# Issuing the stores of the kept dense tiles from ScalarE's queue instead of SyncE's

## The chip, the cores and the metric

The kernel runs on one core of one Trainium2 chip. The metric is the device time of one execution in microseconds (us); the lower, the better. The kernel before was timed three times, and its median is what the changed kernel is compared with. Engines are named TensorE (PE in the profile), VectorE (DVE), ScalarE (ACT), GpSimd (POOL) and SyncE (SP).

## The reference, cut to what matters

Two graph layers run on 6,250 nodes of 128 features. The 106,250 edges are sorted by destination.

```
edge_index = stack([src, dst])
h = relu(layernorm(x));  x = x + GCN(h)      # two convolutions; each gathers rows by src,
                                             # scales them and sums them by dst
h = relu(layernorm(x));  x = x + CFConv(h)   # filter from edge_attr (64 -> 128 -> 128),
                                             # times gathered rows, mean by dst, two linear layers
```

The kernel folds the two weight matrices of the first layer into one, so that what is left of that layer is twice the same thing: out[dst] += table[src] over all edges. These are the first and the second pass. The third pass is the edge filter of the second layer.

## The kernel before, in words

**Two ways to sum.** The 208 groups of 512 edges are sorted by destination. Of every 13 groups, 7 make a dense tile: a matrix of counts between all source nodes (49 blocks of 128) and the 232 destination columns from the tile's first destination on. Such a tile is summed by multiplying the table, held in SBUF as three bf16 parts, with this matrix (`multiply`, L2078). The groups outside tiles are summed by gathering their rows with GpSimd (L1019) and multiplying them with a one-hot matrix (`sum_window`, L2012).

**Building a tile.** A tile has 28 chunks of 128 edges. For each chunk VectorE makes one-hot codes (L1585), TensorE counts them into PSUM (`count_chunk`, L2035 and L2040), and ScalarE copies the counts into the matrix `adjacency` (`copy_chunk`, L1178). The counts have two PSUM places, so TensorE may count chunk m when chunk m-2 has been copied (`wait(pe, chunk_copied, m - 1)`). `adjacency` has two buffers. Before a tile is built, ScalarE zeroes the last columns of its buffer (`clear`, L1157).

**Kept tiles.** 12 of the 16 tiles (`KEPT`) are built in the first pass and needed again in the second. Each is stored to HBM in 7 pieces of 406 KB (`keep`, L787), and loaded again in the second pass (`load_tile`, L798). The store adds to `tile_kept[b]`; for that semaphore `clear` waits when the buffer is to be used again, and SyncE waits once before the second pass.

**The order of the work.** The first pass has 124 slots, one for each group that is gathered. A plan written before anything runs says what belongs to each slot: about 3 chunks of the next tile, a third of a slot's product pieces between them, one or two `pack` steps of the edge attributes for the third pass, and at times a node update. Each engine goes through the slots in order and takes its own part of each, so all five keep in step by semaphores alone. Tiles begin about every 9 slots: the slot in which a tile's last 4 chunks are copied ends with ScalarE's `clear` for the tile that is begun, and has no product on TensorE. The pieces to keep stand in the four slots after that one (2, 2, 2 and 1 pieces):

```
for i in range(PARTS):
    plan.keeps.setdefault(at[t + 1] + 1 + i // 2, []).append((t, i))
```

**SyncE in a slot of the first pass:** loads of edge attributes (`load_attr`, L769, after a wait for TensorE's `packed`), then the pieces to keep (each after a wait for `chunk_copied`), then the store of packed attributes (L781) and the store of the last updated row block (`store_row`, L746).

**ScalarE in a slot of the first pass:** the fields of the next pack (`edge_fields`, L1207), the register loads of the chunks' columns (L1166), the first chunk's copy, `pack_out` (L1221, four copies of 67x64, with its own register loads at L1215), the other chunks' copies, at three places in the pass a zeroing of a packing buffer (L1202, 3.1 us), and `clear` where the plan has one.

**The second and the third pass** have their own loops; the change does not touch their code.

Of the kernel before, what the change touches and what calls it, by code (L numbers as in the profile page):

```python
# [26 lines left out]
COLS = 232  # L27
TILE_GROUPS = 7
TILE_CHUNKS = TILE_GROUPS * CHUNKS
# [48 lines left out]
def gnn_kernel(nc, x, src, dst, edge_attr, edge_weight, W1, b1, W2, b2,  # L78
# [178 lines left out]
    with ExitStack() as ctx:  # L257
# [416 lines left out]
        def _(sp):  # L674
# [106 lines left out]
                sp.dma_start(packed_attr[:, run * SUPER:(run + 1) * SUPER],  # L781
                             packed_T[0:R, run % 2, 0:SUPER]).then_inc(attr_stored[run % 2], 16)

            def keep(t, i):
                b = buffer_of(1, KEPT[t])
                sp.wait_ge(chunk_copied, TILE_CHUNKS * (t + 1))
                sp.dma_start(kept_tiles[t][:, i * BP * COLS:(i + 1) * BP * COLS],  # L787
                             adjacency[:, b, i * BP:(i + 1) * BP, :].rearrange("p b n -> p (b n)")
                             ).then_inc(tile_kept[b], 16)

            def load_tile(order, i):
                t = KEPT.index(PLAN[2].tiles[order])
                before = LOADED.index(order)
# [23 lines left out]
            def fast_path():  # L817
                store_inverse(0)
                for c in (1, 2):
                    plan = PLAN[c]  # L820
                    before = -1
                    if c == 2:
                        sp.wait_ge(block_used[1], NB * len(KEPT))
                        for b in range(2):
                            sp.wait_ge(tile_kept[b], 16 * PARTS * len([t for t in range(len(KEPT)) if t % 2 == b]))
                        wait_stored(sp, 2)
                        load_table(PARTS - 1)
                        sp.wait_ge(inv_stored, 16)
                        load_x(2, 0)
                        for i in range(PARTS):  # L830
                            load_tile(LOADED[0], i)
                    for n in range(SLOT_COUNT[c]):
                        for q in plan.attrs.get(n, []):
                            load_attr(q)
                        for piece in plan.keeps.get(n, []):
                            keep(*piece)
                        if c == 1 and n == max(plan.adds):
                            for i in range(PARTS - 1):
                                load_table(i)
                        for piece in plan.loads.get(n, []):  # L840
                            load_tile(*piece)
                        if n in plan.ends:
                            store_packed(plan.ends[n])
                        if c == 1 and n - 1 in plan.updates:
                            store_row(1, plan.updates[n - 1])
                        if c == 2 and n in plan.updates:
                            j = plan.updates[n]
                            if j:
                                store_mid(j - 1)
                                store_row(2, j - 1)  # L850
                            if j + 1 < NB:
                                load_x(2, j + 1)
                        if c == 2 and n == LAST_PACK_SLOT + 4:
                            for b in range(2):
                                sp.wait_ge(attr_stored[b], 16 * SUPERS // 2)
                            sp.wait_ge(packed_read, SUPERS)
                            late_params()
                        if c == 2 and n == SLOT_COUNT[2] - REST_SLOTS + 2:
                            sp.wait_ge(block_used[2], NB * TILES)
                            for i in range(2):  # L860
                                load_piece(i)
                    if c == 1:
                        left = [plan.updates[SLOT_COUNT[1] - 1]] if SLOT_COUNT[1] - 1 in plan.updates else []
                        for j in left + plan.tail:
                            store_row(1, j)
                    else:
                        first = NB - len(plan.tail)
                        for j in range(first - 1, NB):
                            if j >= first and j + 1 < NB:
                                load_x(2, j + 1)  # L870
                            store_mid(j)
                            store_row(2, j)
# [184 lines left out]
        def _(act):  # L1057
# [135 lines left out]
            def split_middle(b):  # L1193
                source, parts = half_blocks(b)
                act.wait_ge(rest_ready, b + 1)
                nc.scalar.copy(parts[1], source).then_inc(middle_ready, 1)

            def zero_packed(run):
                if run >= 2:
                    act.wait_ge(attr_stored[run % 2], 16 * (run // 2))  # L1200
                    act.wait_ge(packed_read, run - 1)
                nc.scalar.copy(packed_T[:, run % 2, :], zeros[0:RF, 0:1].to_broadcast([RF, WIDE])  # L1202
                               ).then_inc(packed_zero, 1)
# [46 lines left out]
            def fast_path():  # L1250
# [3 lines left out]
                for c in (1, 2):  # L1254
# [3 lines left out]
                    for n in range(SLOT_COUNT[c]):  # L1258
# [36 lines left out]
                        if c == 1 and n in (PARTS, PARTS + 1):  # L1295
                            if n == PARTS:
                                act.wait_ge(parts_ready, 2 * PARTS)
                            zero_packed(n - PARTS)
                        if n in plan.clears:
                            clear(plan.clears[n])  # L1300
                last = SLOT_COUNT[2] - 1
# [1014 lines left out]
```

## Time and profile before

| what | value |
|---|---|
| median of 3 runs | 1527.09 us (1525.73 to 1532.16) |
| profiled execution, first to last instruction | 1923.0 us |
| PE busy | 1426.5 us |
| POOL busy | 1110.3 us |
| DVE busy | 826.7 us |
| ACT busy | 692.3 us |
| mean granted clock of TensorE | 0.850 |

The profiled execution is 396 us longer than the median of the runs; there is no other time of it than this span. So a time from the trace is one of a slower execution: a sum of such times stands against 1923.0 us, and has to be brought to 1527.09 us (a factor of 0.794) before it says anything of the metric. Matmuls are pipelined, and their ends are modelled, so a busy TensorE is not one at its peak. Instructions that load registers, wait, or issue DMAs are not counted as busy; the rows call them ACTq or SPq.

### The profile page before, as it was taken

To read this page: it belongs to the slowest core of one execution; us is meant where nothing else is said; L and a number is where in the kernel's file an instruction comes from. 1 tells how busy PE (TensorE), PEld (TensorE's weight loads), DVE (VectorE), ACT (ScalarE), POOL (GpSimd) and SP (SyncE) were. 2 spreads that over 40 slices of the span, in tenths; PEclk is the share of its full clock that TensorE was granted. 3 is DMA by queue.
4 is the path that set the end of the run, shared out by engine and by line. 5 is a ranking of instruction groups with operands and counts; after the bars stand their busy time and mean duration, and the time that the engine had idled before them with its cause. 6 is when DMAs were issued, how large, how long until landed. Compare 5 with 4: busy or idle time off the path is not lost.

```text
span 1923.0 us, 36276 instructions
## 1 busy us (share of the span) xinstructions
PE 1426.5 (74%) x12042; PEld 1188.7 (62%) x12042; DVE 826.7 (43%) x2907; ACT 692.3 (36%) x1947; POOL 1110.3 (58%) x1150
## 2 busy tenths in 40 slices
PE   3247777888788788885677777767777477888887
PEld 1246666777677676774567666666666345565665
DVE  4854434455445554444133334333333324444444
ACT  3645545555445555442243223322331011111111
POOL 7666656555655655653655555565555645556552
PEclk9856999888988988886899878988998668788887
DMA  3324344444344434447466645664564522344321
GB/s 102 85 52 119 91 118 145 132 133 118 97 130 145 133 110 107 130 132 219 114 162 182 179 125 147 173 183 124 164 179 112 127 63 66 90 98 97 90 71 49
DMA packets 248261, 235.42 MB, mean 122 GB/s; under 512 B 137443, under 2 KB 207512, under 8 KB 247173
## 3 DMA queue, kind: packets, MB, share of 16 engines
q1 hardware_dynamic: 206853, 148.54, 27.9%
q0 software_dynamic: 41216, 84.48, 16.4%
q8 instruction: 101, 1.65, 0.4%
q14 instruction: 91, 0.75, 0.1%
HBM read 173.22 MB, written 59.68 MB: 121 GB/s over the span
## 4 chain that ended last, share of the span: by engine, by line
PE 51%; another core or an unknown queue 15%; issue 12%; DVE 12%; ACT 5%; ACTq 1%; DMA 1%; DVEq 1%; SPq 1%; POOL 0%
PE ps_product L2078 16%; PE ps_banks L2035 6%; PE ps_pack L2052 4%; PE ps_banks L2040 4%; PE ps_banks L2012 4%; PE ps_banks L2195 3%; ACT adjacency L1178 3%; PE ps_banks L2125 2%; PE ps_banks L2206 2%; ACT packed_T L1221 2%; PE ps_banks L2016 2%; PE ps_product L2187 1%; PE ps_pack L2187 1%; DVE code_onehot L1585 1%
## 5 line engine op out<-in xcount | busy, mean ns | idle before, releaser
L1019 POOL DMA_INDIRECT ring_parts<-node_table,src_idx x880 | 852.9, 969 | 612.8 <-issue 208.8
L2078 PE MATMUL ps_product<-adjacency,table_parts 128*128 128x232 bf16 x4116 | 554.2, 283 | 22.2 <-issue 16.9
L2078 PEld LDWEIGHTS ps_product<-adjacency,table_parts 128*128 128x128 bf16 x4116 | 423.1, 108 | 59.6 <-issue 26.7
L1178 ACT CAST adjacency<-ps_banks 128x550 f32 x448 | 298.6, 667 | 389.2 <-PE ps_banks L2040 214.4
L1019 POOL DMA_INDIRECT ring_parts<-node_table,packed_src x216 | 204.4, 946 | 154.1 <-issue 54.2
L2035 PE MATMUL ps_banks<-code_onehot,lo_onehot 128*128 128x300 bf16 x896 | 215.8, 326 | 69.0 <-issue 33.5
L1221 ACT COPY packed_T<-ps_pack 67x64 f32 x832 | 173.8, 209 | 225.7 <-remote 66.9
L1585 DVE TENSOR_SCALAR code_onehot<-code_iota,code_T 128x600 bf16<-128x600 bf16 x448 | 164.6, 383 | 190.4 <-PE ps_banks L2040 142.3
L2052 PE MATMUL ps_pack<-pack_onehot,edge_in 128*67 128x64 f32 x1664 | 165.1, 246 | 51.7 <-ACT edge_in L1207 21.5
L2052 PEld LDWEIGHTS ps_pack<-pack_onehot,edge_in 128*67 128x67 f32 x1664 | 141.7, 160 | 59.4 <-issue 57.6
L2012 PE MATMUL ps_banks<-onehot,ring_parts 128*128 128x64 f32 x992 | 149.8, 300 | 26.6 <-issue 18.8
L2012 PEld LDWEIGHTS ps_banks<-onehot,ring_parts 128*128 128x128 f32 x992 | 140.5, 218 | 30.6 <-issue 30.3
L2035 PEld LDWEIGHTS ps_banks<-code_onehot,lo_onehot 128*128 128x128 bf16 x896 | 91.7, 122 | 92.2 <-issue 59.3
L2040 PEld LDWEIGHTS ps_banks<-code_onehot,lo_onehot 128*128 128x128 bf16 x864 | 103.7, 120 | 34.7 <-issue 7.0
L2040 PE MATMUL ps_banks<-code_onehot,lo_onehot 128*128 128x25 bf16 x864 | 115.9, 222 | 1.9 <-issue 0.7
L1576 DVE TENSOR_TENSOR acc<-acc,ps_banks 128x64 f32 x220 | 47.4, 216 | 149.3 <-PE ps_banks L2016 83.7
L1560 DVE TENSOR_TENSOR pack_onehot<-iota_b,rank 128x256 f32<-128x256 bf16 x208 | 86.9, 418 | 54.9 <-remote 34.0
L1668 DVE SCALAR_TENSOR_TENSOR z_row<-ps_node,dinv,b_all 128x128 f32<-128x128 f32 x47 | 16.5, 350 | 196.7 <-remote 128.9
L1779 DVE SCALAR_TENSOR_TENSOR ring_parts<-ps_banks,packed_dst,ring_parts 128x128 f32<-128x128 f32 x216 | 60.7, 343 | 89.1 <-PE ps_banks L2125 32.4
L1793 DVE TENSOR_TENSOR acc<-acc,ps_banks 128x64 f32 x216 | 47.8, 221 | 107.8 <-PE ps_banks L2195 52.5
L1560 DVE TENSOR_TENSOR onehot<-iota_b,rel 128x256 f32<-128x256 bf16 (+1 forms) x220 | 90.7, 413 | 2.8 <-issue 2.8
L2103 PE MATMUL ps_node<-ident,z_row 128*128 128x128 f32 x47 | 18.0, 383 | 95.0 <-DVE z_row L1681 52.2
(281 smaller groups left out, 1677.6 us busy)
## 6 DMA issues: line engine op xcount, KB each, us to landing
kept_tiles<-adjacency SPq DMA_DIRECT2D x84, 406.0 KB
adjacency<-kept_tiles SPq DMA_DIRECT2D x84, 406.0 KB
edge_in<-in_edge_attr_dram SPq DMA_DIRECT2D x207, 128.0 KB
ring_parts<-node_table,src_idx POOLq DMA_INDIRECT x880
packed_attr<-packed_T SPq DMA_DIRECT2D x8, 864.0 KB
adjacency<-packed_attr SPq DMA_DIRECT2D x6, 1152.0 KB
node_table<-row_space SPq DMA_DIRECT2D x49, 96.0 KB
table_parts<-node_table SPq DMA_DIRECT2D x7, 672.0 KB
```

The source lines that it names most:

```text
L1019: gps.indirect_dma_start(to, None, table[c], bass.IndirectOffsetOnAxis(index, 0)).then_inc(gathered[s], 16)
L1178: nc.scalar.copy(adjacency[:, b, :, bass.ds(at, n)].rearrange("p (t b) n -> p t b n", t=2), chunk_banks(m).rearrange("p t (b n) -> p t b n ...
L1221: nc.scalar.copy(packed_T[:, run % 2, bass.ds(at[k], WINDOW)], ps_pack[0:RF, k * WINDOW:(k + 1) * WINDOW]).then_inc(packed_out, 1)
L1560: return vec.tensor_tensor(to, iota[:], of.unsqueeze(2).to_broadcast([P, CHUNKS, WINDOW]), ALU.is_equal)
L1585: vec.tensor_scalar(code_onehot[:, m % CODE_SETS, :], code_iota[:], code_T[:].bitcast(F32)[:, at:at + 1], None, ALU.is_equal).then_inc(chu ...
L1779: last = vec.scalar_tensor_tensor(out=ring[:, s, k, :], in0=ps_filter[:, h % 2, k * P:(k + 1) * P], scalar=packed_cut[:, CHUNKS * h + k:CH ...
L2012: last = mm(to, ring[:, s, k, :], onehot[:, half, k, :], start=(k == 0), stop=(k == CHUNKS - 1))
L2035: last = mm(chunk_banks(m)[:, half, :], left(m), code_onehot[:, m % CODE_SETS, half * HIGH * SPAN:(half + 1) * HIGH * SPAN], start=True, s ...
L2040: last = mm(chunk_banks(m)[:, half, :].rearrange("p (b n) -> p b n", n=SPAN)[:, :, 0], left(m - 1), shared.rearrange("p (b n) -> p b n", n ...
L2052: last = mm(ps_pack[0:RF, k * WINDOW:(k + 1) * WINDOW], edge_in[:, s, k, :], pack_onehot[:, q % 2, k, :], start=True, stop=True)
L2078: product = mm(ps_product[:, 0:COLS], table_parts[:, k, part, :], adjacency[:, buffer_of(c, tile), k, :], start=(k == 0 and part == 0), st ...
L2195: last = mm(ps_agg[:, h % 2, k * WINDOW:(k + 1) * WINDOW], ring[:, h % SLOTS, k, :], onehot[:, h % 2, k, :], start=True, stop=True)
```

## The change

`keep` moves from SyncE's program to ScalarE's, word for word but for the engine that waits and issues. On SyncE it stood behind the slot's attribute loads; on ScalarE it stands at the end of the slot, behind the last chunk's copy, the last `pack_out` and the zeroing of a packing buffer, and ahead of `clear`. The plan is the same, and so are the 84 transfers, their sizes and the semaphores.

```diff
@@ block.sync
-            def keep(t, i):
-                b = buffer_of(1, KEPT[t])
-                sp.wait_ge(chunk_copied, TILE_CHUNKS * (t + 1))
-                sp.dma_start(kept_tiles[t][:, i * BP * COLS:(i + 1) * BP * COLS],
-                             adjacency[:, b, i * BP:(i + 1) * BP, :].rearrange("p b n -> p (b n)")
-                             ).then_inc(tile_kept[b], 16)
...
                         for q in plan.attrs.get(n, []):
                             load_attr(q)
-                        for piece in plan.keeps.get(n, []):
-                            keep(*piece)
@@ block.scalar
+            def keep(t, i):
+                b = buffer_of(1, KEPT[t])
+                act.wait_ge(chunk_copied, TILE_CHUNKS * (t + 1))
+                nc.scalar.dma_start(kept_tiles[t][:, i * BP * COLS:(i + 1) * BP * COLS],
+                             adjacency[:, b, i * BP:(i + 1) * BP, :].rearrange("p b n -> p (b n)")
+                             ).then_inc(tile_kept[b], 16)
...
                             zero_packed(n - PARTS)
+                        for piece in plan.keeps.get(n, []):
+                            keep(*piece)
                         if n in plan.clears:
                             clear(plan.clears[n])
```

## Rows read from the trace of the kernel before

**Rows 1.** The page: span, busy times, and the chain by engine.

```profile
span 1923.0 us, 36276 instructions
PE 1426.5 (74%) x12042; PEld 1188.7 (62%) x12042; DVE 826.7 (43%) x2907; ACT 692.3 (36%) x1947; POOL 1110.3 (58%) x1150
PE 51%; another core or an unknown queue 15%; issue 12%; DVE 12%; ACT 5%; ACTq 1%; DMA 1%; DVEq 1%; SPq 1%; POOL 0%
```

**Rows 2.** Busy time by stretch, first to last piece kept (179.8 to 850).

```profile
core 0: us, PE busy (x) PEld busy (x) DVE busy (x) ACT busy (x) POOL busy (x), PEclk, DMA share, GB/s
179.80:850.00 670.20, 538.47 (x4900) 472.64 (x4899) 314.39 (x1064) 341.25 (x902) 396.15 (x409) 0.90 0.44 127
```

**Rows 3.** The same for the 12 stretches in which pieces are stored.

```profile
295.60:310.20 14.60, 13.32 (x129) 11.43 (x129) 8.94 (x35) 6.85 (x14) 8.01 (x9) 0.93 0.94 295
...
sum 202.90, PE 172.64 PEld 154.70 DVE 111.95 ACT 112.94 POOL 121.75; mean PE 14.39 PEld 12.89 DVE 9.33 ACT 9.41 POOL 10.15
```

**Rows 4.** Who PE waited for, 170 to 850: us, times, longest.

```profile
PE ps_pack L2052 <- ACT edge_in L1207: 21.3, 10, 3.3
PE ps_banks L2035 <- ACT adjacency L1178: 21.2, 34, 2.3
...
PE ps_pack L2052 <- ACT packed_T L1221: 11.8, 9, 4.8
```

**Rows 5.** Who POOL and DVE's row code waited for, 170 to 850.

```profile
POOL ring_parts L1019 <- PE ps_banks L2012: 125.4, 60, 5.5
...
POOL ring_parts L1019 <- remote: 57.0, 43, 2.1
...
DVE z_row L1635 <- PE ps_node L2089: 31.2, 23, 3.9
```

**Rows 6.** Who SP's queue waited for, 170 to 850.

```profile
SPq L769 <- PE ps_pack L2052: 239.2, 56, 14.0
SPq L769 <- remote: 180.4, 32, 11.1
SPq L787 <- ACT adjacency L1178: 46.9, 18, 7.0
```

**Rows 7.** All store issues: ns min/median/max, first and last start.

```profile
L787 SPq DMA_DIRECT2D kept_tiles<-adjacency x84: 338/452/2217, 179.8 to 845.5; - x84
```

**Rows 8.** SP in order of time, the tenth tile's first pieces: start, us, what.

```profile
709.28 0.81 SPq L787 DMA_DIRECT2D kept_tiles<-adjacency  x2
710.14 0.50 SPq L746 DMA_DIRECT2D node_table<-row_space  x1
```

**Rows 9.** ACT in order of time, from the clear ahead of those pieces; idle before in brackets.

```profile
709.12 2.19 ACT L1157 CAST adjacency<-zeros 128x2400 bf16<-128x2400 f32 x1
...
714.95 0.62 ACT L1178 CAST adjacency<-ps_banks 128x550 f32 x1 [0.25 <-PE ps_banks L2040]
715.47 0.21 ACT L1207 COPY edge_in<-fields 128x12 f32<-128x12 f32 x1
716.55 0.81 ACT L1178 CAST adjacency<-ps_banks 128x550 f32 x1 [0.88 <-PE ps_banks L2040]
```

**Rows 10.** ACT, the first tile's same place, and the last tile's.

```profile
186.89 0.81 ACT L1178 CAST adjacency<-ps_banks 128x550 f32 x1
...
836.86 0.62 ACT L1178 CAST adjacency<-ps_banks 128x550 f32 x1 [2.65 <-issue]
```

**Rows 11.** PE in order of time, the slot after, with chunks 1 and 3.

```profile
715.92 0.42 PE L2035 MATMUL ps_banks<-code_onehot,lo_onehot 128*128 128x300 bf16 x2
...
718.87 0.42 PE L2035 MATMUL ps_banks<-code_onehot,lo_onehot 128*128 128x300 bf16 x2
```

**Rows 12.** ACT's groups, 179.8 to 850: count, busy, mean ns, idle before.

```profile
L1178 ACT CAST adjacency<-ps_banks 128x550 f32 (+1 forms) x316 | 210.7, 667 | 263.3 <-PE ps_banks L2040 159.5 <-remote 67.2 <-issue 27.9
```

**Rows 13.** The chain that ended last, 179.8 to 850, by line.

```profile
by line: PE ps_product L2078 16.0%; PE ps_banks L2035 12.3%; another core or an unknown queue 12.1%; issue 9.7%; PE ps_banks L2040 9.0%; PE ps_banks L2012 8.0%; PE ps_pack L2052 7.3%; ACT adjacency L1178 6.4%; ACT packed_T L1221 3.3%; DVE c
```

**Rows 14.** DMA queues, 295.6 to 310.2: packets, MB, share of 16 engines.

```profile
q1 hardware_dynamic: 1891, 3.79, 81.1%
q0 software_dynamic: 239, 0.50, 12.6%
```

## The prediction, written before the changed kernel ran

> **What bounds the kernel.** I read the page first: the span, the busy times and the chain of work that ended last [rows 1]. TensorE is busy for 1426.5 of 1923.0 us and holds half of the chain, and another 27% of the chain is time that no instruction filled (an unknown releaser or "issue"). The unprofiled runs take 1527.09 us, little more than TensorE's busy time, so I take it that there most of these unfilled stretches are gone, and that the kernel is bound by TensorE's own work. ScalarE, the engine that gets new work, is busy for 692.3 us.
>
> Then I read only the stretch where the change acts, from the first store to the last. It has 670.2 us, of which TensorE is busy for 538.5, GpSimd for 396.2 and ScalarE for 341.3 [rows 2]. The 12 stretches in which pieces are stored have 202.9 us together, with ScalarE busy for 112.9 of them [rows 3], and one of them stands as example.
>
> Third, who waits for whom. TensorE waited for ScalarE for 21.3 + 21.2 + 11.8 = 54.3 us, in 53 pieces [rows 4]: it is not idle for long, but ScalarE does reach it. GpSimd waits for TensorE, 125.4 us, not for a transfer, and VectorE's row code waits for TensorE too [rows 5]. In the full lists of waits of this stretch no engine that computes waits for a DMA. SyncE waits nearly always: 419.6 us ahead of the attribute loads, and 46.9 us, in 18 pieces, ahead of the stores that now move [rows 6].
>
> **What is removed from SyncE.** 84 issues with a median of 452 ns [rows 7], so 84 x 0.452 = 38.0 us, and the 46.9 us of waits for `chunk_copied` [rows 6]. Behind a store on its queue stand the store of an updated row and the next attribute load; in the tenth tile the row store was issued 0.05 us after a pair of pieces ended [rows 8]. Both now go out up to some us earlier. Who would gain? TensorE's packs, if they waited for attributes, and VectorE, if it waited for a free row buffer. Neither wait is in the lists [rows 4, 5]: the loads are issued three packs ahead and the rows have three buffers. I count this at 0. If that cover were thinner than the lists show, the gain would be bounded by what is taken off SyncE; I price it as a rival.
>
> **What is added to ScalarE.** The 84 waits are met when they are reached: the last chunk of a tile is copied by ScalarE itself one slot earlier. The issues cost ScalarE's queue what they cost SyncE's: 38.0 us, or 84 x 0.338 = 28.4 us by the shortest [rows 7]. They come as pairs, 2 x 0.452 = 0.90 us, in three of the four slots after a clear, and as a single one in the fourth. What hides a pair? It stands between the slot's last copy and the next slot's attribute fields. Take the tenth tile [rows 9]. The last copy started at 714.95, and the next instruction of ScalarE started 0.52 us later. The queue is free while a copy runs, so the first 0.52 us of the pair lie under that copy, and 0.90 - 0.52 = 0.38 us delay the fields. Behind them ScalarE was idle for 0.88 us, until TensorE had counted the next chunk. So the pair fits in with 0.50 us to spare.
>
> That is the first place after the clear, which itself takes 2.19 us [rows 9] and puts ScalarE behind. I looked at this same place in all 12 tiles: the idle time there went from none (the first tile) to 2.65 us (the last) [rows 10]; seven of the 12 had 0.88 us or more, the other five 0.24 us or less. In one of these five a zeroing of 3.1 us stands ahead of the pair and covers it. In the other four the pair delays the first copy of the next slot by up to 0.38 us, together under 1.5 us.
>
> Does a late first copy reach TensorE? It counts chunk m only after the copy of chunk m-2, so this copy is wanted when the slot's third chunk comes. TensorE began the slot's first chunk at 715.92 and the third at 718.87 [rows 11], 2.95 us later, while a copy takes 0.67 us [rows 12]. A delay of 0.38 us is inside that. It comes through only where ScalarE is behind already. Its chain has a measure for that: of the chain in this stretch ScalarE's copies hold 6.4 + 3.3 = 9.7% [rows 13]. With this share of the issues exposed, the cost is 0.097 x 38.0 = 3.7 us. The bounds are 0 (every pair hidden, as in the tenth tile) and 38.0 us (none hidden); I take 3.7, near the lower one, since seven of 12 places are wide.
>
> The next user of the buffer is the other thing that a later store could hold up. The pieces now go out about one slot later, at the end of ScalarE's slot. The clear that waits for them stands five slots after the last piece, and the second pass waits for them nine slots after the last tile's last piece. The first piece belongs to slot 13 and the last to slot 115, so a slot is 670.2 us / 102, or 6.6 us, and one slot of delay is hidden by four: 0.
>
> **The transfers.** They are the same. In a stretch of stores the 16 engines are nearly full: 81.1% for SyncE's queue and 12.6% for GpSimd's [rows 14]. The stores will now be on a second hardware queue, and share the engines with the attribute loads instead of standing ahead of them. GpSimd's gathers have the 125.4 us of waiting for TensorE as cover [rows 5]. I count 0.
>
> **The sum.** 0 + 3.7 + 0 + 0 = +3.7 us on the profiled 1923.0 us, times 1527.09 / 1923.0 = 0.794: +2.9 us. The forecast is 1527.1 + 2.9 = 1530.0 us, slower by 0.2%. A measurement of this kernel can tell about 0.5% (7.6 us) from no change, so I expect no visible difference. This case reaches from 1524 to 1534.
>
> **Rival 1: ScalarE falls behind after each clear and the issues are exposed.** For it: the slot with the clear has four chunks and no product, the lightest slot for TensorE and the heaviest for ScalarE; TensorE's waits for it are 54.3 us already [rows 4]; and an issue took up to 2.2 us when the engines were full [rows 7], nearly as long as the clear. In the unprofiled run the idle places may also be narrower than in the trace. Against it: seven of 12 wide places. The point from which it decides is a delay over the about 1.5 us that TensorE leaves between its wish for the copy and the copy's normal end. Price: the first pair of each tile, 12 x 0.90 = 10.8, times 0.794 = 8.6 us: 1536. With every issue exposed 38.0 x 0.794 = 30.2 us: 1557. Half of that is 1542. Chance 24%.
>
> **Rival 2: two hardware queues with work crowd GpSimd's gathers.** In the stretch of [rows 14] GpSimd's queue gets 12.6% beside 81.1%. The page DMA: Bandwidth & Descriptors of the Trainium skill, section Queues, rings and completion order, says that each DMA engine goes round the queues that have work, packet by packet; by this rule a second hardware queue lowers a gather's share while both are full. No row shows two hardware queues of data at once, so the trace neither agrees nor disagrees. In this kernel it would look so: a gather lands late, TensorE's `sum_window` waits at L2012. It decides once a gather is later than GpSimd's lead; GpSimd waited for TensorE 60 times, 2.1 us in the mean [rows 5]. With 1 us lost per tile in 12 tiles, 12 x 0.794 = 9.5 us: 1537. Chance 6%.
>
> **Rival 3: it gets faster, because SyncE is free.** 46.9 + 38.0 = 84.9 us are taken off SyncE. If part of the chain's unnamed time (12.1% [rows 13]) is work that waited for SyncE, the gain is 0.121 x 84.9 = 10.3, times 0.794 = 8.2 us: 1519. Against it stand the lists without a wait for a transfer. The Trainium skill has a rule on its side, in Perfetto Trace Analysis, section DMA Optimizations: if generating descriptors is the bottleneck, spreading DMAs over the engines that can issue them may help. The condition is not met here: SyncE mostly waits for TensorE [rows 6]. By the rule's words alone one would expect a gain; by the trace none. Chance 10%.
>
> **How the numbers follow.** The forecast's case has 60%, rivals 1, 2 and 3 have 24, 6 and 10. So faster by over 0.5%: 0.10; within 0.5%: 0.60; slower: 0.24 + 0.06 = 0.30. The range starts at 1518, which takes in rival 3's price, and ends at 1548, which takes in rival 2 and rival 1 up to two thirds of its full price. I leave out about 5% below and 8% above.
>
> **What would show it.** In the changed kernel's profile: 84 store issues on ScalarE's queue with a median near 0.45 us; SyncE's wait for `chunk_copied` gone; idle time of ScalarE ahead of L1178 less by about 30 us, where it was named as a wait for TensorE; TensorE's waits for L1178, L1207 and L1221 up by less than 5 us from 54.3. Rival 1 would show as these waits 10 us or more higher, or as issues of 1 us and more on ScalarE. Rival 2 would show as waits of TensorE at L2012 for a DMA, which the trace of before does not have here. Rival 3 would show as a shorter first pass with the same waits for ScalarE. I am wrong if the unprofiled kernel has its ScalarE less idle than the trace lets one think: nothing in the trace measures that, and the factor of 0.794 spreads evenly what need not be even.

## The result, and the profile of the kernel after

The changed kernel takes 1558.2 us (median of 4 runs, 1555.7 to 1560.7); the kernel before, run beside it, takes 1526.4 us (1522.8 to 1532.2). The ratio is 1.0196, with a 95% interval of 1.0164 to 1.0228: slower by 2.0%, 31.8 us, where 0.2% was forecast. The time lies outside the forecast's range.

First the page of the kernel after: span, busy times, three DMA queues, the chain by engine and the start of it by line.

```profile
span 1558.9 us, 36276 instructions
PE 1270.3 (81%) x12042; PEld 1102.8 (71%) x12042; DVE 832.3 (53%) x2907; ACT 693.5 (44%) x1947; POOL 1114.7 (72%) x1150
...
q1 hardware_dynamic: 194757, 113.61, 28.0%
q0 software_dynamic: 41216, 84.48, 20.0%
q10 hardware_dynamic: 12096, 34.93, 6.1%
...
PE 39%; POOL 17%; issue 12%; DVE 9%; ACT 9%; ACTq 7%; DMA 5%; SPq 1%; DVEq 0%; POOLq 0%
```

Beside [rows 1] two things differ. The stores are on a queue of their own now: q10 moves 34.93 MB. And ScalarE holds 9% + 7% of the chain instead of 5% + 1%, its queue (ACTq: instructions that load registers, issue and wait) the 7%. But the span beside [rows 1] would make the kernel after 364 us faster. That can't be compared, and so the first experiment takes a second profile of the kernel before. Its span is 1528.0 us, close to its time, and its page reads:

```profile
span 1528.0 us, 36275 instructions
PE 1271.4 (83%) x12041; PEld 1108.2 (73%) x12042; DVE 829.1 (54%) x2907; ACT 693.9 (45%) x1947; POOL 1117.4 (73%) x1150
...
PE 48%; POOL 18%; issue 13%; DVE 11%; DMA 4%; ACT 3%; SPq 1%; ACTq 1%; DVEq 1%; POOLq 0%
```

Every engine is busy for the same time in both, within 0.5%. So the 31 us are waiting, not work. Where are they? The store issues, and under them the loads of the same pieces in the second pass, of the kernel before (second profile) and of the kernel after (count, ns min/median/max, first and last start):

```profile
L787 SPq DMA_DIRECT2D kept_tiles<-adjacency x84: 338/442/2512, 157.7 to 683.3; - x84
L798 SPq DMA_DIRECT2D adjacency<-kept_tiles x84: 319/327/503, 737.6 to 1135.2; - x84
```

```profile
L1192 ACTq DMA_DIRECT2D kept_tiles<-adjacency x84: 326/327/2002, 164.2 to 720.4; - x84
L791 SPq DMA_DIRECT2D adjacency<-kept_tiles x84: 319/327/504, 766.4 to 1165.0; - x84
```

From the first to the last store it is 525.6 us before and 556.2 after: 30.6 us more, nearly the whole loss, in the stretch that the prediction looked at. The last load of the second pass is issued at 1135.2 and 1165.0, 29.8 us apart: nothing more is lost or won there. The waits of this stretch (150 to 720 us: who waited for whom, us in total, times, longest), first in the kernel before, second profile:

```profile
POOL ring_parts L1019 <- issue: 133.2, 437, 0.3
POOL ring_parts L1019 <- PE ps_banks L2012: 2.1, 7, 0.3
...
PE ps_banks L2035 <- ACT adjacency L1178: 16.8, 19, 1.6
...
ACT adjacency L1178 <- PE ps_banks L2040: 116.5, 107, 4.4
...
ACT adjacency L1178 <- issue: 8.6, 16, 1.7
```

and then in the kernel after:

```profile
POOL ring_parts L1010 <- issue: 122.8, 402, 0.5
POOL ring_parts L1010 <- PE ps_banks L2012: 31.3, 27, 5.3
...
PE ps_banks L2035 <- ACT adjacency L1169: 54.7, 53, 1.9
...
ACT adjacency L1169 <- PE ps_banks L2040: 76.1, 60, 6.6
ACT adjacency L1169 <- issue: 56.4, 35, 3.2
```

Read them from the bottom up. ScalarE's copies no longer wait so long for TensorE's counts (116.5 to 76.1 us) but for "issue", that is for ScalarE's own queue (8.6 to 56.4). TensorE waits 37.9 us more for these copies. And GpSimd, whose gathers need a place that TensorE has read, waits for TensorE for 31.3 us instead of 2.1: 29.2 us more, the size of the loss.

GpSimd's own line says what bounds this stretch. It is busy for 400.65 of the 525.6 us of the second profile (by the stretch's busy times), and waits about 0.30 us at "issue" ahead of each gather. A slot has four gathers at 976 ns (mean of all gathers of the run): 4 x (0.976 + 0.30) = 5.1 us, and the stretch has 525.6 / 102 = 5.15 us a slot. So GpSimd sets the pace of the first pass, and it has no spare time; the others may be late by as much as their lead and no more. This is read from its waits; no run makes the gathers themselves faster.

What does ScalarE's queue do in those 56.4 us? The chain that ended last, in the stretch of 255 to 275 us of the kernel after (start, us, what):

```profile
by line: ACTq L1157 35.2%; ACT adjacency L1169 24.2%; ACTq L1192 11.8%; ACT adjacency L1148 10.3%; issue 9.7%; ACT packed_T L1219 7.0%; ACTq L1213 3.1%; ACT edge_in L1205 3.1%; ACTq L1169 2.1%; ACTq L1219 1.7%; ACTq L591 0.5%
...
260.25 1.76 ACTq L1192
262.05 0.21 ACT edge_in L1205
262.26 3.06 ACTq L1157
...
267.72 0.57 ACTq L1192
268.29 0.04 issue
268.33 0.20 ACT edge_in L1205
268.54 2.02 ACTq L1157
```

The issues of the pieces (L1192) hold 11.8%. Three times as much, 35.2%, is L1157: the loads of the chunks' columns into ScalarE's registers (L1166 before). Such a load stands next on the queue behind a pair, with only the short fields copy (L1205) between them. Two single ones, right behind a pair and three slots later where no store is about:

```profile
L1157 ACTq TENSOR_LOAD <-chunk_at x1: 3254/3254/3254, 262.1 to 262.1; - x1
L1157 ACTq TENSOR_LOAD <-chunk_at x1: 697/697/697, 284.4 to 284.4; - x1
```

Now all column loads from 130 to 730 us, each by itself. The 48 right behind a store issue of ScalarE took 1.23 to 3.25 us, together 91.1; the 63 others have a median of 0.70. All together are 132.4 us, and 102.1 in the second profile of the kernel before. That sum already holds slow loads: where hardly any meets the pieces it is 79 to 80 us (e2 and e8 below), and in the kernel before single loads took up to 2.61 us while SyncE's pieces moved. So ScalarE's queue was given 36.8 us of issues and 30.3 us of longer loads: 67 us, of which about 30 came through.

### The profile page after: what moved, and what is told of

It is laid out like the page before. It is cut to its first block, busy times and chain, and to the rows that moved or that the text cites. A ratio compares the mean times of both kernels' runs of the same rounds, so it can differ in the third digit from the quotient of the medians.

```text
span 1558.9 us, 36276 instructions
## 1 busy us (share of the span) xinstructions
PE 1270.3 (81%) x12042; PEld 1102.8 (71%) x12042; DVE 832.3 (53%) x2907; ACT 693.5 (44%) x1947; POOL 1114.7 (72%) x1150
## 3 DMA queue, kind: packets, MB, share of 16 engines
q10 hardware_dynamic: 12096, 34.93, 6.1%
## 4 chain that ended last, share of the span: by engine, by line
PE 39%; POOL 17%; issue 12%; DVE 9%; ACT 9%; ACTq 7%; DMA 5%; SPq 1%; DVEq 0%; POOLq 0%
PE ps_product L2078 18%; POOL ring_parts L1010 17%; PE ps_pack L2052 4%; ACT adjacency L1169 4%; PE ps_banks L2035 4%; PE ps_banks L2012 4%; ACTq L1157 4%; ACT packed_T L1219 3%; ACTq L1213 2%; PE ps_banks L2016 1%; DMA ring_parts<-node_table,packed_src 1%; PE ps_banks L2040 1%; DMA src_raw<-in_src_dram 1%; ACTq L1192 1%; DMA ring_parts<-node_table,src_idx 1%
## 5 line engine op out<-in xcount | busy, mean ns | idle before, releaser
L2078 PE MATMUL ps_product<-adjacency,table_parts 128*128 128x232 bf16 x4116 | 502.3, 268 | 0.0
L2078 PEld LDWEIGHTS ps_product<-adjacency,table_parts 128*128 128x128 bf16 x4116 | 398.9, 102 | 11.5
L2035 PE MATMUL ps_banks<-code_onehot,lo_onehot 128*128 128x300 bf16 x896 | 199.7, 308 | 61.3 <-ACT adjacency L1169 55.8
L1585 DVE TENSOR_SCALAR code_onehot<-code_iota,code_T 128x600 bf16<-128x600 bf16 x448 | 169.8, 391 | 124.5 <-PE ps_banks L2040 122.3
L2012 PE MATMUL ps_banks<-onehot,ring_parts 128*128 128x64 f32 x992 | 144.8, 295 | 21.2 <-issue 10.2
L2052 PE MATMUL ps_pack<-pack_onehot,edge_in 128*67 128x64 f32 x1664 | 146.0, 233 | 11.5 <-ACT packed_T L1219 6.6
L2012 PEld LDWEIGHTS ps_banks<-onehot,ring_parts 128*128 128x128 f32 x992 | 136.4, 213 | 24.9 <-issue 23.7
L2035 PEld LDWEIGHTS ps_banks<-code_onehot,lo_onehot 128*128 128x128 bf16 x896 | 90.9, 120 | 77.6 <-issue 37.8
L2052 PEld LDWEIGHTS ps_pack<-pack_onehot,edge_in 128*67 128x67 f32 x1664 | 126.3, 148 | 15.5 <-issue 10.9
L2016 PE MATMUL ps_banks<-onehot,ring_parts 128*128 128x64 bf16 x1152 | 52.2, 198 | 60.5 <-issue 30.1
L1779 DVE SCALAR_TENSOR_TENSOR ring_parts<-ps_banks,packed_dst,ring_parts 128x128 f32<-128x128 f32 x216 | 60.8, 344 | 65.7 <-DMA ring_parts<-node_table,packed_src 49.1
L2016 PEld LDWEIGHTS ps_banks<-onehot,ring_parts 128*128 128x128 bf16 x1152 | 46.7, 101 | 68.2 <-issue 58.7
```

The lines of the kernel that those rows point to most:

```text
L1585: vec.tensor_scalar(code_onehot[:, m % CODE_SETS, :], code_iota[:], code_T[:].bitcast(F32)[:, at:at + 1], None, ALU.is_equal).then_inc(chu ...
L2012: last = mm(to, ring[:, s, k, :], onehot[:, half, k, :], start=(k == 0), stop=(k == CHUNKS - 1))
L2016: last = mm(to, ring_parts[:, s, k, part * F:(part + 1) * F], onehot_b[:, half, k, :], start=(k == 0 and part == 0), stop=(k == CHUNKS - 1 ...
L2035: last = mm(chunk_banks(m)[:, half, :], left(m), code_onehot[:, m % CODE_SETS, half * HIGH * SPAN:(half + 1) * HIGH * SPAN], start=True, s ...
L2052: last = mm(ps_pack[0:RF, k * WINDOW:(k + 1) * WINDOW], edge_in[:, s, k, :], pack_onehot[:, q % 2, k, :], start=True, stop=True)
L2078: product = mm(ps_product[:, 0:COLS], table_parts[:, k, part, :], adjacency[:, buffer_of(c, tile), k, :], start=(k == 0 and part == 0), st ...
```

## The experiments

All times are medians, and each ratio is to the kernel before run beside it. "Loads" are ScalarE's column loads from 130 to 730 us, all durations added (114 loads, and 107 to 111 in the slowest kernels); "GpSimd" is what GpSimd waited for TensorE from 150 to 720 us.

| kernel | us | ratio, 95% interval | loads, us | GpSimd, us |
|---|---|---|---|---|
| before, second profile (e1) | 1529.8 | same kernel | 102.1 | 2.1 |
| after | 1558.2 | 1.0196 [1.0164, 1.0228] | 132.4 | 31.3 |
| e2 SyncE issues at ScalarE's moment | 1530.3 | 1.0007 [0.9988, 1.0026] | 79.3 | 2.1 |
| e3 small stores on ScalarE besides | 1535.2 | 1.0032 [1.0010, 1.0053] | 90.3 | 1.8 |
| e4 after, column load ahead of the stores | 1530.9 | 1.0008 [0.9986, 1.0030] | 81.7 | 2.4 |
| e5 SyncE issues, ScalarE waits for it | 1566.0 | 1.0238 [1.0203, 1.0274] | 128.4 | 32.4 |
| e6 ScalarE delayed, no DMA moved | 1566.5 | 1.0255 [1.0228, 1.0281] | 86.6 | 40.7 |
| e7 after, one piece a slot | 1534.1 | 1.0037 [1.0022, 1.0053] | 133.7 | 3.4 |
| e8 after, stores right behind the load | 1527.5 | 1.0000 [0.9986, 1.0015] | 79.8 | 2.1 |
| e9 after, each load reads four | 1567.5 | 1.0263 [1.0236, 1.0290] | 137.8 | 49.1 |
| e10 before, column load ahead | 1528.8 | 1.0004 [0.9987, 1.0022] | 100.9 | 2.7 |
| e11 after, loads of whole fours | 1538.0 | 1.0061 [1.0037, 1.0084] | 77.6 | 4.9 |

**e1, the kernel before again.** No edit.

> The kernel before, unchanged, for a second profile: the first one has a span of 1923 us against a median of 1527 us. All theories expect a time near 1527 us. If the profiled span comes near that too, the stretches with an unknown releaser (15% of the chain) should be gone, and its first pass can be laid beside that of the changed kernel, whose span is 1558.9 us. Expected first pass, from first to last store: about 530 us, against 556 us in the changed kernel.

What it showed stands above: [rows 1] to [rows 14] come from an execution of 1923 us in which GpSimd waited for TensorE for 125.4 us [rows 5]; in one of 1528 us it is 2.1. The cover that the prediction gave GpSimd from these rows does not exist in the timed kernel.

**e2, SyncE issues at ScalarE's moment.** Is it the moment of the stores, a slot later, or their queue?

```
-                sp.wait_ge(chunk_copied, TILE_CHUNKS * (t + 1))
+                sp.wait_ge(keep_turn, PARTS * t + i + 1)
...
+                        for t, i in plan.keeps.get(n, []):
+                            act.wait_ge(chunk_copied, TILE_CHUNKS * (t + 1))
+                            act.sem_inc(keep_turn, 1)
...
```

> SyncE issues the stores again, but not before ScalarE has come to the place where the changed kernel issues them (ScalarE adds 1 to a semaphore there). Traffic at the changed kernel's moments, issue on the old engine. Theory L (the register load of chunk columns that stands right behind the issues on ScalarE's queue is slow, 1.4 to 3.3 us instead of 0.7): near the kernel before, 1527 +- 6 us, column loads back to 0.7 us. Theory T (these loads are slow because the DMA engines are full, whoever issued): near the changed kernel, 1553 to 1560 us. Theory I (84 issues of 0.33 us, 27.5 us, lie bare on ScalarE): 1527 +- 6 us.

Measured: 1530.3, no difference. The moment of the stores costs nothing. ScalarE went on at once here, and its load began together with SyncE's issue: it was short (median 706 ns, 79.3 us in all). Theory T, as this expectation words it (1553 to 1560 us), missed. But the load had ended before the data moved: by the DMA records of the kernel after, the first packet of a pair comes 0.85 us (median) behind the start of the pair's first issue. So e2 does not settle T, and e5 tests it with a load that does meet the data.

**e3, the issues alone.** SyncE stores the pieces as before. ScalarE issues 84 stores of 16 bytes on each of 128 partitions at the places where the kernel after has its pieces; they carry nothing that is used.

```
+                nc.scalar.dma_start(tiny[t][:, i * 4:(i + 1) * 4], zeros[:, 0:4]).then_inc(tiny_stored, 16)
...
+                        for piece in plan.keeps.get(n, []):
+                            keep_tiny(*piece)
```

> SyncE stores the tiles as in the kernel before; ScalarE issues, where the changed kernel issues its stores, 84 other stores of 128 rows of 16 bytes each from a constant tile. Issue on ScalarE without the traffic. Theory I: as slow as the changed kernel, 1553 to 1560 us. Theory T: little changes, 1527 to 1533 us, column loads as in the kernel before. Theory L: 1550 us or more if the mere issue ahead makes the load slow, 1530 to 1540 us if the load has to wait for the bytes or the descriptors of its own queue's transfers.

The issues cost ScalarE what the real ones cost it:

```profile
L1202 ACTq DMA_DIRECT2D tiny<-zeros x84: 326/327/2089, 164.9 to 696.5; - x84
```

Measured: 1535.2, +0.32%, some 5 us, 2 above what theory T gave and inside theory L's second range. By its interval it is 1.5 to 8 us, the size of the prediction's 2.9 us. (The column loads were 12 us shorter in sum than in e1, so this is not the issues quite alone.) Issues on ScalarE cost about what was said; what the loss of 31.8 us needs besides is something that comes with the data.

**e4, the column load ahead of the stores.** In the kernel after, ScalarE loads the columns of the next slot before it issues this slot's stores and clears. Nothing is taken out of its queue.

```
...
-                        counted = list(zip(counted, chunk_columns(counted)))
+                        counted = list(zip(counted, columns))
...
+                        columns = chunk_columns(plan.onehots.get(n, []))
                         for piece in plan.keeps.get(n, []):
                             keep(*piece)
```

> The changed kernel, with the register load of the next slot's chunk columns taken ahead of the slot's stores (and ahead of the clear). Same stores, same place, but the nearest register load behind them is now that of the pack, behind the next slot's first copy. Theory L: most of the loss comes back, 1527 to 1540 us. Theory I: nothing comes back, 1553 to 1560 us. Theory T: about half, since loads behind a pair still meet the traffic of the pair before: 1538 to 1550 us.

Measured: 1530.9, no difference from before; loads 81.7 us, GpSimd's waits back to 2.4. With 84 issues on ScalarE's queue and the load in front of them, the loss is gone. So the cause lies in the order "issue, then load".

**e5, whose queue is it?** Two theories were left. T: a register load is slow while the pieces' data move, whoever issued them. Q: it is slow behind an issue on the same queue. Here SyncE issues, and ScalarE only waits until it has.

```
...
+                sp.sem_inc(keep_issued, 1)
...
+                        for t, i in plan.keeps.get(n, [])[-1:]:
+                            act.wait_ge(keep_issued, PARTS * t + i + 1)
```

> SyncE issues the stores at ScalarE's moment, as in the run that did so before, but ScalarE now waits until SyncE has issued the slot's pieces before it goes on to the column load. So ScalarE's load begins, as in the changed kernel, behind the issues and while the stores' data move, only the issues are not on its own queue. Theory Q (a register load waits for transfers of its own queue): column loads 0.7 us, time 1530 to 1538 us (the cost of standing still during the issues). Theory T (a register load is slow while the stores' data move, whoever issued them): column loads of 1.2 to 3.2 us behind 48 stops, time 1553 to 1562 us.

Measured: 1566.0, +2.4%, 4 us above T's range and far from Q's. No store is on ScalarE's queue, and the 48 loads behind SyncE's issues took 1.23 to 2.56 us, 87.4 together (91.1 after). Q falls, T holds.

**e6, is a delay of ScalarE enough?** The kernel before, with six copies of 128x16, one waiting for the other, at the end of each of the 48 slots with pieces. No DMA is moved.

```
+                        if n in plan.keeps:
+                            for _ in range(6):
+                                link(nc.scalar.copy(idle_out[:], zeros[:, 0:16]))
```

> The kernel before, with six linked copies of 16 columns on ScalarE at the end of each of the 48 slots in which stores are due: about 1.5 us each time, 72 us in all, without a DMA. That is the size of what the changed kernel adds to ScalarE there (36.8 us of issues and about 30 us of longer column loads). If delay of ScalarE is all there is to the loss: 1550 to 1565 us. If it is not (the loss comes from transfers on two queues, or from something late elsewhere): 1527 to 1540 us.

In each of the 48 slots the six copies took 1.38 to 1.40 us, 66.6 us together, as much as the 67 of the kernel after. Measured: 1566.5, +2.6%, with shorter loads (86.6 us) and GpSimd's waits at 40.7 us. The delay alone does it: no crowding of the DMA engines is needed for the loss. That it costs 7 us more than the change did (and ends 1.5 us above the expected range) is not explained; the copies spread the delay otherwise over pairs and single pieces.

T can be looked for elsewhere in the traces. Three lines of the second profile of the kernel before: one column load of the first pass, the store of packed attributes that SyncE had issued 0.8 us ahead of it, and all column loads of the second pass, in which the same 84 pieces are loaded from HBM instead of stored:

```profile
L1166 ACTq TENSOR_LOAD <-chunk_at x1: 2553/2553/2553, 378.9 to 378.9; - x1
L781 SPq DMA_DIRECT2D packed_attr<-packed_T x1: 456/456/456, 378.2 to 378.2; - x1
L1166 ACTq TENSOR_LOAD <-chunk_at x36: 485/498/747, 778.3 to 1114.6; - x36
```

The one load was slow without any piece near it, behind another store, and the same load took 1.8 to 3.7 us in 12 of the 13 runs (0.31 in e11). The loads of the second pass, of two or three columns, took 0.49 to 0.75 us; the one at 969 us took 0.49 while packets of a piece on its way in held 95% of the DMA engines' time. So it is transfers out of SBUF that go with slow loads here, not full DMA engines as such.

**e7 and e8, two other places.** e7 spreads the seven pieces over seven slots (`+ 1 + i` for `+ 1 + i // 2`). e8 issues the pairs right behind the slot's column load, ahead of its first copy.

```
                         counted = list(zip(counted, chunk_columns(counted)))
+                        for piece in plan.keeps.get(n, []):
+                            keep(*piece)
...
-                        for piece in plan.keeps.get(n, []):
-                            keep(*piece)
```

> The changed kernel with one piece in each of seven slots instead of 2, 2, 2 and 1 in four. A column load behind a single issue took 1.25 to 1.4 us in the changed kernel, behind a pair up to 3.25. The sum over all slots hardly changes (84 x (0.33 + 0.6) = 78 us against 96 us), but each slot can absorb its 0.9 us. Theories Q and T both: 1532 to 1545 us; if the sum of delays alone counts: 1550 us or more.

> The changed kernel with the slot's stores issued right behind its column load and ahead of its first copy. The next register load is that of the pack (0.3 us), behind that copy, about 1 us after the issues. If a load is slow for as long as the pair's data move (812 KB, about 2 us at the 400 GB/s that the trace shows in such stretches), the pack's loads become slow, to 1 us or more, and the time lies between, 1535 to 1552 us. If only a load with nothing between it and the issue is slow: 1527 to 1536 us.

Measured: e7 1534.1 (+0.37%), e8 1527.5 (1.0000). In e7 the loads behind a piece are as many as 84 and long (median of all 1.28 us, 133.7 in all), and with 27.4 us of issues ScalarE is given 27.4 + (133.7 - 102.1) = 59 us, hardly less than the 67 of the kernel after. Yet GpSimd waits only 3.4 us. What counts is how much falls into one slot: about 0.7 us in each of 84 slots is hidden, about 1.4 us in each of 48 (67 / 48) is not. In e8 the full 37.3 us of issues are on ScalarE, in pairs, and nothing is lost: the next column load comes a slot later. The expectation had asked about the loads of `pack_out`, which come first behind the stores there. They did become slow, as T wants: 35 of them took more than 0.4 us, up to 1.27, and their sum from 130 to 730 us rose from 45.2 us (e1) to 58.1. The time that was to go with it, 1535 to 1552 us, did not come: these 13 us were hidden. In e4 it was the same (55.7 us).

**e9 and e11, what a load consists of.** Away from stores a load of two columns took 0.49 us, of three 0.70, the 4-column loads of `pack_out` 0.31. So I let every column load read four.

```
+                start = min(at, NT - 4)
                 _, columns = nc.values_load_multi_w_load_instructions(
-                    chunk_at[0:1, at:at + len(chunks)], engines=[ACTIVATION], min_val=0, max_val=COLS - SPAN,
+                    chunk_at[0:1, start:start + 4], engines=[ACTIVATION], min_val=0, max_val=COLS - SPAN,
...
-                return columns
+                return columns[at - start:at - start + len(chunks)]
```

> The kernel after, in which each column load of ScalarE reads four columns in one instruction, where the kernel after reads three in most slots; the extra one is not used. A load of four took 0.305 us in every run so far and one of three 0.70 us, so loads are short by 114 x 0.4 = 45 us in the first pass. Theory T (a column load that runs while a store's pieces move takes 1.2 to 3.3 us, and this is what holds up ScalarE) with the further idea that three columns are read one after another, each read being stretched: the load behind a pair takes a third of 1.9 us, 0.4 to 0.8, GpSimd's waits for TensorE fall from 31.3 to under 5 us, and the time is that of before, 1524 to 1534. If instead the load is held back by a fixed time whatever it reads, it takes 1.2 to 2.8 us behind a pair still; the other loads are 0.4 us shorter, which gives back 0.4 of every slot's time on ScalarE, and the time is 1535 to 1550.

Measured: 1567.5, +2.6%, slower still. Both answers of the expectation miss. Four loads of e9 show why; the first two stand right behind stores, the other two don't.

```profile
L1158 ACTq TENSOR_LOAD <-chunk_at x1: 3012/3012/3012, 213.1 to 213.1; - x1
L1158 ACTq TENSOR_LOAD <-chunk_at x1: 312/312/312, 231.4 to 231.4; - x1
L1158 ACTq TENSOR_LOAD <-chunk_at x1: 907/907/907, 236.2 to 236.2; - x1
L1158 ACTq TENSOR_LOAD <-chunk_at x1: 309/309/309, 249.7 to 249.7; - x1
```

The nine slots of most tiles begin at chunks 0, 3, 6, 9, 12, 15, 18, 21 and 24 (`spread(28, 9)`). Away from stores the loads at 0 and 24, multiples of four, took 0.31 us and those at 15, 18 and 21 took 0.91 us. Of the 46 loads behind a store from 130 to 730 us, the 11 at chunk 12, the second line above among them, took 306 to 315 ns, and the other 35 took 1.6 to 4.2 us. In the kernel after, the same loads at chunk 12 read three columns, and took 1.25 to 1.42 us. That points to the number of separate reads instead of the number of columns. But the loads at chunk 12 all stand behind a single piece, and by the DMA records of e9 its first packet came 0.50 to 0.55 us behind the end of the issue: a load of 0.31 us was over by then, and says nothing of a read that meets the data. e11 therefore loads whole fours from a multiple of four, one or two of them, and uses three of the values:

```
+                start, stop = at // 4 * 4, -(-(at + len(chunks)) // 4) * 4
...
+                    chunk_at[0:1, start:stop], engines=[ACTIVATION], min_val=0, max_val=COLS - SPAN,
```

> The kernel after, in which ScalarE's column load takes whole groups of four columns that begin at a multiple of four: one group (4 values) or two (8 values), of which the slot's three are used. In the run that read four columns from wherever the slot began, a load of four that began at a multiple of four took 0.31 us, beside a store too (306 to 315 ns), and one that began elsewhere took 0.91 us alone and 2.3 to 4.2 us behind a store. Theory G (four values that begin at a multiple of four are read at once, any others one by one, and each single read is what a store stretches): loads of 4 take 0.31 us and of 8 take 0.5 to 0.7 us, behind a store not over 1.3; GpSimd's waits for TensorE fall from 31.3 to under 8 us, and the time is 1524 to 1535. Rival N (it is the number of values alone): loads of 8 take 1.7 us alone and 4 us and more behind a store, and the time is 1580 or more.

Two single loads of e11 away from stores, one of one four and one of two, and one of two fours behind a pair:

```profile
L1158 ACTq TENSOR_LOAD <-chunk_at x1: 307/307/307, 194.3 to 194.3; - x1
L1158 ACTq TENSOR_LOAD <-chunk_at x1: 542/542/542, 190.1 to 190.1; - x1
L1158 ACTq TENSOR_LOAD <-chunk_at x1: 2017/2017/2017, 260.4 to 260.4; - x1
```

Eight values take 0.54 us, less than three read one by one (0.70): theory G holds there, and N falls. But behind a pair it was too hopeful: a load of one four took 0.7 to 1.2 us there and of two up to 2.02, where 1.3 was the most expected; the 48 loads behind a store sum to 50.9 us. The time is 1538.0, 3 us beyond the expected range, and +0.6% is left of +2.0%. The order of the queue being that of the kernel after, shorter loads alone give back about two thirds of the loss.

**e10, the same cure on the kernel before.** ScalarE's column load is put at the end of the slot ahead, as in e4.

> The kernel before with nothing changed but the place of ScalarE's column load: it is issued at the end of the slot ahead, in front of that slot's clear, as in the run that cured the changed kernel. If the first pass is paced by GpSimd's gathers (it waited 2.1 us for TensorE in all), a better place of the load gives nothing: 1522 to 1532. If ScalarE still set part of the pace before, it gives up to the 16.8 us that TensorE waited for it: 1510 to 1520.

Measured: 1528.8, no difference. TensorE's 16.8 us of waits for ScalarE are not on the path: GpSimd sets the pace of the first pass, and a better ScalarE gives it nothing.

No version beat the kernel before by more than can be measured; e8, e4, e2 and e10 are all equal to it.

## Why the prediction was wrong, by its own steps

**What bounds the kernel: wrong for the stretch that matters.** The prediction named TensorE. In the second profile GpSimd is never held up in the first pass (2.1 us), and TensorE is busy for 481.9 of 525.6 us. The 125.4 us that GpSimd waited for TensorE [rows 5] were taken as cover; they belonged to the long execution. A span 396 us above the time of the runs should have barred every reading of cover from this trace, not only a reading of durations, which the factor of 0.794 was made for. The prediction's last sentences say so, and drew no price from it.

**What is removed from SyncE, 0: right.** The wait for `chunk_copied` left SyncE's queue, and its waits for TensorE ahead of the attribute loads (L769) grew from 363.4 to 449.3 us. e2, which delays SyncE's stores, changes nothing either.

**What the issues cost ScalarE, 38.0 us: right.** They took 36.8 us in sum, with a median of 327 ns instead of the 452 foreseen, and their exposed part, by e3, is some 5 us, against 2.9 foreseen.

**"The pair fits in with 0.50 us to spare": here it failed.** This step counted the 0.88 us that ScalarE was idle behind the fields [rows 9] as free. Register loads are not counted as busy, and one stood exactly there. The row of the trace of before that the step lacked:

```profile
L1166 ACTq TENSOR_LOAD <-chunk_at x1: 1162/1162/1162, 715.0 to 715.0; - x1
```

The load ran from 715.0 to about 716.2, under the copy and the fields, and the next copy began at 716.55. It needs the queue, and a pair ahead of it moves it: 715.0 + 0.90 + 1.16 = 717.1, which is 0.5 us behind the start of the next copy, where the prediction had 0.50 us to spare. The copy's tolerance of 1.5 us would still have held that in this one tile, but the term for ScalarE then is not the issues alone. The term "added to ScalarE" was 38.0 us and measured 67: it left out that the load goes from lying beside a running copy to lying behind the pair, and that it is slow there, 1.9 us in the mean of the 48 (+30.3 us over all loads).

The count of "seven of 12" wide places failed for the same reason. In the trace of before the load took 1.05 to 2.35 us in the seven wide places and 0.69 to 0.71 us in the five narrow ones; by the DMA records, packets of SyncE's own pieces held 73 to 95% of the DMA engines' time during the seven and 0 to 44% during the five. The place was wide because the load in it was slow, and it was no room:

```profile
L1166 ACTq TENSOR_LOAD <-chunk_at x1: 2242/2242/2242, 657.3 to 657.3; - x1
```

**"With this share of the issues exposed", 9.7%: wrong too.** About 30 of 67 us came through, 45%. e7 shows that no fixed share can be right: 59 us in smaller portions lost some 6 us (e7, +0.37%).

**Transfers and buffers, 0 and 0: right.** TensorE's waits at L2012 for a DMA are not among the first ten in the kernel after; rival 2's sign is missing. GpSimd's busy time in the stretch rose only from 400.65 to 405.52 us, for 418 gathers instead of 411. That the stores go out later costs nothing (e2, e8).

**The rivals.** Rival 1, ScalarE falls behind and it shows as waits of TensorE, gave 1557 for all issues exposed, beside the 1558.2 measured, and its sign came: TensorE waits 37.9 us more for the copies. But the sum agrees by accident. Its mechanism was the issues, which make up about 5 us of the 32 (e3), and the load behind them does the rest (e4, e5). Its place was right: the slots behind each clear. Rival 3, a gain by a free SyncE, fell: no engine had waited for it.

The Trainium skill has a figure for register loads, in Runtime: NRT & Kernel Launch, section Instruction fetch mechanics: about 200 ns per register, even in bulk, since each load is a round trip. The page speaks of the runtime's own loads from HBM; these read SBUF. The trace agrees for the second and third register (0.49 and 0.70 us for two and three), and disagrees for four from a multiple of four (0.31 us) and beside a store (up to 3.25 us for three). An estimate from the page's figure alone, 48 loads of three at 0.6 us, is 29 us behind the stores, a third of the 91.1 measured.

What stays open: why a register load on ScalarE's queue is slow while pieces move. The runs show that the queue that issued does not matter (e5), that small stores do not do it (e3), that pieces on their way in do not (the second pass), and that fewer separate reads make the load shorter (e11). How much must be moving is open too: in e7, with one piece at a time, the four-column loads of `pack_out` kept their 0.31 us with one exception (0.52), while the three-column loads took 1.3. Where the read waits, at SBUF or on its way, no run shows.

## What to carry to other kernels

An engine's idle time in a list of its busy instructions is not free: look for register loads, waits and issues of its queue in it before you put something there, and price what stands right behind the new instruction, since it loses the cover under which it ran. In this kernel a register load belonged ahead of a large store, not right behind it (e4, e8). And ask first which engine has no wait at all in the stretch: the lead of the others over it, slot by slot, is the room that a moved instruction has, and a sum over the stretch does not say whether it fits.

## What the runs showed of the hardware

- A register load of three values from SBUF took 0.70 us alone and 1.2 to 3.3 us right behind the issue of one or two 406 KB stores, also when SyncE had issued them (1.2 to 2.6 us). While the same pieces were loaded from HBM, loads of two or three values took at most 0.75 us.
- One of four values from a multiple of four took 0.31 us, of eight 0.54 us, of three 0.70 us, of four from elsewhere 0.91 us. Behind a pair of stores the four from a multiple of four took 0.7 to 1.2 us.
- A store's issue took ScalarE's queue 327 ns (median), SyncE's 442 ns, for the same pieces; but 339 ns on SyncE where it issued them at ScalarE's moment (e2), so the difference is not shown to be the engine's.
- The first profiled execution of the kernel before took 1923 us and the second 1528, while TensorE, VectorE, ScalarE and GpSimd did the same instructions.
